# The normed rows of a graph layer turned by 32 x 32 blocks on VectorE and through DRAM, not by matmuls

## The chip, the cores and the metric

The kernel runs on one core of one Trainium2 chip. The time is the device time of that core in microseconds. The kernel before takes 1281.36 us, the median of three runs (1281.25 to 1281.46).

## The reference

Sixty-four graphs of 128 nodes with 256 features go through three layers with an attention over the neighbours and a feed-forward network:

```
h = relu(layernorm(x))                       # per node, 256 features
for l in range(3):
    si, sj = h @ attn_w[l, :256], h @ attn_w[l, 256:]
    scores = leaky(si[:, :, None] + sj[:, None, :] + attn_b[l])    # leaky slope 0.2
    attn = softmax(where(adj or diagonal, scores, -inf))           # 128 x 128 per graph
    y = layernorm(h + attn @ h) * g1[l] + beta1[l]
    ff = gelu(y @ W1[l] + b1[l]) @ W2[l] + b2[l]                   # 256 -> 1024 -> 256
    h = layernorm(y + ff) * g2[l] + beta2[l]
out = x + h
```

## The kernel before, in words

**Items and slots.** An item is four graphs in one layer (512 tokens); there are 48. Item q has layer q % 12 // 4, so four items of layer 0, four of layer 1 and four of layer 2 follow one another. Each engine's queue is written out by hand: a prologue for items 0 to 3, and then a function `slot(s)` for each s, in which an engine works on several items at once. In it `t` is item s - 1 (its second norm and output), `f` is item s (its feed-forward), `b` item s + 1, `a` item s + 2 and `d` item s + 3 (attention), and `p`, item s + 4, whose input is loaded and normed if it is of layer 0. Engines meet at semaphores alone, and each engine runs its queue in order.

**TensorE.** `ffn1(i, c)` makes 128 of the 1024 hidden features for 512 tokens: six matmuls of 512 columns (both operands split into a high and a low part) into one of three banks `hbank`. `ffn2(i, c)` adds that chunk's share of the output: twelve matmuls of 256 columns into two banks `acc`. An item's eight chunks of both are spread over a slot, and between them stand `e_turn` (four transposes of the exponentials E), `aggregate` (eight records, E by the rows x) and `z1_turn` (two times four transposes of the normed rows z, since ffn1 wants the features on the partitions). `e_turn` and `z1_turn` write the one bank `util`. `acc` has four banks, two for an item, so that one item's sums stand while the next item's are made; `aggregate` writes the banks of its item before ffn2 does.

**ScalarE.** `gelu_high` (gelu and a rounded copy) for each chunk, `h_high` (scale, shift and rounded copy of the turned z in `util`), `leaky`, `exps`, `et_out` (copy of the turned E), `first_x` (the input norm applied). Gelu and exp lie in different tables, so there are two table loads in a slot.

**VectorE.** `low` (the low part of a hidden chunk), `h_low` (the low part of the turned z), `j_dots` and `i_dots` (the products with the two attention vectors, four for each), `masked` (mask and sj row into the scores, one instruction), `minus_max`, `attend` (x plus the aggregate), `residual` (y plus ff), moments and norms. `variance` also adds epsilon (`ve`).

**GpSimd.** The power -0.5 (`make_rstd`) and the products and sums with the gamma and beta rows: `h_gamma`, `h_beta`, `x_gamma`, `x_beta`, `add_input`, each on two graphs (128x512). `h_gamma(i, h)` writes the ring `hb` of two items, and so waits for `residual(i - 2, h)`.

**DMA.** All DMAs stand in SyncE's queue. `send_sj` puts the sj values (16 bytes for each partition) into DRAM, and `load_sj` brings them back to all partitions.

Of the kernel before, what the change touches and what calls it, by code (L numbers as in the profile page):

```python
# [33 lines left out]
P = 128  # L34
# [12 lines left out]
LEAD = 3  # L47

# [3 lines left out]
def build(nc, x, adj, attn_w, attn_b, W1, b1, W2, b2, g1, beta1, g2, beta2, out):  # L52
# [19 lines left out]
    with ExitStack() as ctx:  # L72
# [27 lines left out]
        ET = sb("ET", [P, GG, P])  # L100
        sj_bc = sb("sj_bc", [P, P, GG])
        sj_dram = nc.dram_tensor("sj_dram", [2, P, GG], F32).ap()
# [8 lines left out]
        dots = sb("dots", [P, 2, GG])  # L111
        si = sb("si", [P, GG])
# [7 lines left out]
        ve = {n: sb(f"ve{n}", [P, GG]) for n in "012"}  # L120
        rstd = {n: sb(f"rstd{n}", [P, GG]) for n in "012"}
# [13 lines left out]
        acc = [psum(f"acc{i}", [P, HG, D]) for i in range(4)]  # L135
        util = psum("util", [P, TOK])

        def acc_of(i, h): return acc[2 * (i.q % 2) + h]
# [28 lines left out]
        zt_n = sem("zt_n")  # L167

# [13 lines left out]
        si_n = sem("si_n")  # L182
        pen_n = sem("pen_n")
        mask_n = sem("mask_n")
        negm_n = sem("negm_n")
# [33 lines left out]

        def x_of(i):  # L220
            return xs[:, i.q % XR]
# [28 lines left out]

        def wait_ring(eng, q):

            if q >= XR:
                eng.wait_ge(zt_n, KD * (q - XR + 1))
                eng.wait_ge(hgam_n, 2 * (q - XR + 1))
# [3 lines left out]
        def _(sp):  # L259
# [32 lines left out]
            def load_adj(i):  # L292
                wait(sp, pen_n, i.g)
                sp.dma_start(adji[:], group(adj, i.g)).then_inc(adj_in, 16)

            def load_weights(n):
                l, w, h = halves[n]
# [4 lines left out]
            def send_sj(i):  # L302
                sp.wait_ge(dotj_n, i.q + 1)
# [3 lines left out]
            def load_sj(i):  # L307
                sp.wait_ge(sj_sent, 16 * i.q)
# [3 lines left out]

            def slot(s):
                t, o, d, p = item(s - 1), item(s - 2), item(s + 3), item(s + 4)
                if p and p.l == 0:
                    load_xraw(p)
                if 6 <= s + 5 < len(halves):
                    load_weights(s + 5)
                if s == ITEMS - 4:
                    sp.wait_ge(x0_n, GG * NG)  # L320
                    sp.dma_start(xraw[:], group(x, NG - 1)).then_inc(last_in, 16)
                if o and o.l == L - 1 and o.q < ITEMS - 1:
                    for h in range(2):
                        gs = slice(h * HG, (h + 1) * HG)
                        sp.wait_ge(out_ready, 2 * o.g + h + 1)
                        sp.dma_start(group(out, o.g)[:, gs], xout[:, o.g % 2, gs]).then_inc(out_sent[o.g % 2], 16)
                if t and t.l == L - 1 and t.q < ITEMS - 1:
                    wait(sp, out_ready, 2 * t.g)
                    if t.g == 0:
                        sp.wait_ge(ln1_ready, 1)  # L330
                    sp.dma_start(xres[:], group(x, t.g)).then_inc(xres_in, 16)
                if p and p.l == 0:
                    load_adj(p)
                if d:
                    send_sj(d)
                    load_sj(d)

            load_xraw(item(0))
# [10 lines left out]
            load_xraw(item(2))  # L349
            load_adj(item(1))  # L350
            load_ln2_rows()
            load_attn_rows(False)
            load_weights(4)
            send_sj(item(1))
            load_sj(item(1))
            load_adj(item(2))
            load_weights(5)
            load_adj(item(3))
            load_xraw(item(3))
            send_sj(item(2))  # L360
            load_sj(item(2))
            for s in range(0, ITEMS + 3):
# [10 lines left out]
        def _(pool):  # L373
# [9 lines left out]
            def make_rstd(n, q):  # L383
                if n == "2" and q == ITEMS - 1:
                    return
                pool.wait_ge(ve_n[n], q + 1)
                if n == "0":
                    wait(pool, x0_n, GG * q)
                pool.tensor_tensor(rstd[n][:], ve[n][:], halfs[:], ALU.pow).then_inc(rstd_n[n], 1)  # L389
# [52 lines left out]
            def last_rstd(i):  # L442
                for h in range(2):
                    gs = slice(h * HG, (h + 1) * HG)
                    pool.wait_ge(ve_n["2"], i.q + h + 1)
# [11 lines left out]
            def slot(s):  # L457
                o, t, f, b, d = item(s - 2), item(s - 1), item(s), item(s + 1), item(s + 3)
                if o and o.l == L - 1:
                    add_input(o, 0)  # L460
                if o:
                    x_beta(o, 1)
                if d and d.l == 0:
                    make_rstd("0", d.g)
                if o and o.l == L - 1:
                    add_input(o, 1)
                if t:
                    make_rstd("2", t.q)
                if f:
                    h_beta(f, 0)  # L470
                if t:
                    x_gamma(t, 0)
                if f:
                    h_beta(f, 1)
                if b:
                    make_rstd("1", b.q)
                    h_gamma(b, 0)
                if t:
                    x_beta(t, 0)
                    x_gamma(t, 1)  # L480
                if b:
                    h_gamma(b, 1)
# [5 lines left out]
            make_rstd("0", i1.g)  # L488
            make_rstd("1", i0.q)
# [618 lines left out]
```

## Time and profile before

| what | value |
|---|---|
| median of three runs | 1281.36 us |
| the profiled execution: its time, its span | 1281.6 us, 1279.8 us |
| TensorE's granted clock, mean | 0.997 of full speed |
| busy: TensorE, VectorE, ScalarE, GpSimd | 97%, 87%, 72%, 51% of the span |
| prologue, until the first ffn1 has its second operand | 34 us |

Busy is the union of an engine's instructions. A matmul's record reaches over the start of the next one, so the distance between starts is what a matmul costs, and a busy share near 100% says that it never waited. The span is 1.8 us shorter than the profiled execution's own time.

### The profile page before, as it was taken

How to read it: one execution, taken by the hardware profiler on the slowest of the kernel's cores; microseconds unless marked ns; L12 is line 12 of the kernel's file. 1: busy time of each engine (PE TensorE's matmuls, PEld its weight loads, DVE VectorE, ACT ScalarE, POOL GpSimd, SP SyncE). 2: the span in 40 equal slices, each digit the busy share in tenths (PEclk: the TensorE clock that was granted, in tenths of full speed). 3: DMA queues.
4: the chain of work that ended last, by engine and by line, in shares of the span. 5: the costliest groups of instructions: out<-in, count | busy, mean ns of one | idle time of the engine just before them, and what ended most of it. 6: DMA issues, size and time to landing. Idle time of an engine off the chain costs nothing.

```text
span 1279.8 us, 23042 instructions
## 1 busy us (share of the span) xinstructions
PE 1240.6 (97%) x7877; PEld 1122.5 (88%) x7877; DVE 1110.3 (87%) x3331; ACT 917.7 (72%) x1754; POOL 652.5 (51%) x535
## 2 busy tenths in 40 slices
PE   3899999999999999999999999999999999999997
PEld 1799999988899999999889999999989899989996
DVE  7888888899998788889998888789999888888765
ACT  4777777677876776678777776777778766776663
POOL 1435553556555534554566445544666355435563
PEclk9999999999999999999999999999999999999998
DMA  7111111112220001011230000002321100000111
GB/s 248 53 33 43 26 26 34 34 51 66 67 67 10 10 10 17 10 34 51 75 100 26 9 18 10 9 10 43 99 75 42 34 10 9 10 17 26 26 41 58
DMA packets 52944, 52.31 MB, mean 41 GB/s; under 512 B 9272, under 2 KB 45148, under 8 KB 52828
## 3 DMA queue, kind: packets, MB, share of 16 engines
q1 hardware_dynamic: 52828, 50.85, 14.4%
q8 instruction: 62, 1.02, 0.3%
q14 instruction: 54, 0.44, 0.1%
HBM read 42.36 MB, written 8.48 MB: 40 GB/s over the span
## 4 chain that ended last, share of the span: by engine, by line
PE 77%; DVE 18%; ACT 2%; issue 2%; DMA 1%; POOL 0%; DVEq 0%; POOLq 0%
PE acc L955 35%; PE hbank L940 33%; PE acc L969 5%; DVE hid_lo L541 3%; PE util L990 3%; DVE xs L680 2%; PE util L1000 1%; DVE xs L667 1%; DVE st L528 1%; DVE st L674 1%; DVE ve L519 1%; DVE mv L517 1%; DVE st L562 1%; DVE junk L627 1%; DVE sc L654 1%
## 5 line engine op out<-in xcount | busy, mean ns | idle before, releaser
L955 PE MATMUL acc<-w2hi,hid_hi 128*128 128x256 f32 x1536 | 446.0, 290 | 0.0
L813 ACT ACTIVATE hbank<-hbank,vec 128x512 f32<-128x512 f32 x384 | 253.7, 661 | 266.5 <-PE hbank L940 262.0
L955 PE MATMUL acc<-w2hi,hid_lo 128*128 128x256 f32 x1536 | 434.9, 283 | 0.0
L955 PE MATMUL acc<-w2lo,hid_hi 128*128 128x256 f32 x1536 | 434.4, 283 | 0.0
L389 POOL TENSOR_TENSOR rstd<-ve,halfs 128x4 f32<-128x4 f32 x111 | 120.1, 1082 | 492.1 <-DVE ve L519 487.2
L940 PE MATMUL hbank<-ht_hi,w1hi 128*128 128x512 f32 x768 | 311.2, 405 | 2.8 <-DVE hid_lo L541 1.4
L955 PEld LDWEIGHTS acc<-w2hi,hid_hi 128*128 128x128 f32 x1536 | 293.8, 191 | 10.5
L940 PE MATMUL hbank<-ht_lo,w1hi 128*128 128x512 f32 x768 | 302.6, 394 | 0.0
L955 PEld LDWEIGHTS acc<-w2lo,hid_hi 128*128 128x128 f32 x1536 | 293.7, 191 | 8.8
L940 PE MATMUL hbank<-ht_hi,w1lo 128*128 128x512 f32 x768 | 300.8, 392 | 0.0
L955 PEld LDWEIGHTS acc<-w2hi,hid_lo 128*128 128x128 f32 x1536 | 293.5, 191 | 0.0
L541 DVE TENSOR_TENSOR hid_lo<-hbank,hid_hi 128x512 fp32r<-128x512 f32 x384 | 257.5, 683 | 26.5 <-ACT hid_hi L819 24.7
L819 ACT CAST hid_hi<-hbank 128x512 fp32r<-128x512 f32 x384 | 225.6, 587 | 13.7 <-PE acc L955 1.7
L409 POOL TENSOR_TENSOR hb<-xs,ln_rows 128x512 f32<-128x512 f32 x96 | 128.9, 1343 | 87.2 <-DVE xs L680 87.2
L940 PEld LDWEIGHTS hbank<-ht_hi,w1lo 128*128 128x128 f32 x768 | 144.7, 188 | 32.6
L940 PEld LDWEIGHTS hbank<-ht_hi,w1hi 128*128 128x128 f32 x768 | 145.7, 190 | 25.6 <-DVE ht_lo L685 2.1
L940 PEld LDWEIGHTS hbank<-ht_lo,w1hi 128*128 128x128 f32 x768 | 145.9, 190 | 19.9
L685 DVE TENSOR_TENSOR ht_lo<-util,ht_hi 128x512 fp32r<-128x512 f32 x96 | 66.2, 689 | 95.1 <-ACT ht_hi L836 95.1
L416 POOL TENSOR_TENSOR hb<-hb,ln_rows 128x512 f32<-128x512 f32 x96 | 124.5, 1298 | 0.0
L680 DVE TENSOR_SCALAR xs<-xs,mv,rstd 128x256 f32<-128x256 f32 x192 | 112.0, 646 | 1.0 <-POOL rstd L389 0.9
L829 ACT ACTIVATE util<-util,vec 128x512 f32<-128x512 f32 x96 | 72.4, 754 | 36.1 <-PE util L990 35.9
L426 POOL TENSOR_TENSOR xs<-xs,ln_rows 128x512 f32<-128x512 f32 x64 | 82.7, 1292 | 23.4 <-DVE xs L570 23.4
(76 smaller groups left out, 1740.3 us busy)
## 6 DMA issues: line engine op xcount, KB each, us to landing
sj_bc<-sj_dram SPq DMA_DIRECT2D x47, 256.0 KB, 3.9
xraw<-in_x_dram SPq DMA_DIRECT2D x16, 512.0 KB, 4.4
out_dram<-xout SPq DMA_DIRECT2D x32, 256.0 KB, 4.4
xres<-in_x_dram SPq DMA_DIRECT2D x15, 512.0 KB, 5.6
xout<-in_L_gnn_W_dram SPq DMA_DIRECT2D x10, 512.0 KB, 5.0
adji<-in_adj_dram SPq DMA_DIRECT2D x16, 256.0 KB, 2.9
ln_rows<-in_L_gnn_g_dram SPq DMA_DIRECT2D x2, 384.0 KB, 8.0
ln_rows<-in_L_gnn_beta_dram SPq DMA_DIRECT2D x2, 384.0 KB, 7.6
```

The costliest lines, as they stand in the source:

```text
L389: pool.tensor_tensor(rstd[n][:], ve[n][:], halfs[:], ALU.pow).then_inc(rstd_n[n], 1)
L409: pool.tensor_tensor(hb[:, i.q % 2, gs], x_of(i)[:, gs], rows_of(ln1_rows[:, 0], i.l), ALU.mult).then_inc(hgam_n, 1)
L416: pool.tensor_tensor(t, t, rows_of(ln1_rows[:, 1], i.l), ALU.add).then_inc(hb_n, 1)
L426: pool.tensor_tensor(t, t, rows_of(ln2_rows[:, 0], i.l), ALU.mult).then_inc(gam_n, 1)
L541: dve.tensor_tensor(hid_lo[:, k % HID], hbank[k % HB][:], hid_hi[:, k % HID].bitcast(F32), ALU.subtract).then_inc(lo_n, 1)
L680: dve.tensor_scalar(x_of(i)[:, g], x_of(i)[:, g], mv["1"][:, g, 0:1], rstd["1"][:, g:g + 1], ALU.subtract, ALU.mult).then_inc(z1_n, 1)
L685: dve.tensor_tensor(ht_lo[:, i.q % 2, m], util[:], ht_hi[:, i.q % 2, m].bitcast(F32), ALU.subtract).then_inc(htlo_n, 1)
L813: act.activation(hbank[k % HB][:], hbank[k % HB][:], ACT.Gelu, bias=b1c(i.l, c)).then_inc(gelu_n, 1)
L819: act.copy(hid_hi[:, k % HID], hbank[k % HB][:]).then_inc(hi_n, 1)
L829: act.activation(util[:], util[:], ACT.Identity, bias=beta1c(i.l, m), scale=g1c(i.l, m)).then_inc(ht_n, 1)
L940: mm = pe.matmul(hbank[k % HB][:], w[:, i.l, m, at_c], v[:, i.q % 2, m], start=m == 0 and n == 0, stop=m == KD - 1 and n == 2)
L955: mm = pe.matmul(to, v[:, k % HID, of_g], w[:, i.l, c], start=c == 0 and n == 0 and g % HG == 0, stop=c == C - 1 and n == 2, skip_group_ch ...
```

## The change

The turned rows of item 0 and 1 are still made by TensorE. For items 2 to 47 VectorE transposes z in 32 x 32 blocks (`turn_z`, one instruction over 128x1024), SyncE writes the result to a DRAM scratch of 512 KB (`send_z`) and reads it back in four DMAs, one for each group of 32 partitions, so that the blocks land turned as a whole in `zt` (`move_z`); `h_out` reads `zt` in place of `util`. `e_turn` writes a bank of the aggregation (`mix`), no longer `util`. The banks are dealt out anew: two `acc` for ffn2, in place of four, and two `mix` for E and the aggregation. So `ffn2(f, 0)` waits for both `residual` of the item before, and aggregation for the `attend` before.

`masked` is four instructions that add the mask and give the row's largest value as well, and `minus_max` works with four values for each partition, no longer with the 128x512 scores; it needs `penalty` to be cut off at 0 by a second instruction. The attention bias goes into `i_dots`. Epsilon is added on GpSimd. `input_shift` is one instruction, not four. And the order of every queue is written anew:

```
     def acc_of(i, h): return acc[h]
     def mix_of(i, h): return mix[h]
...
+            def send_z(i):
...
+                sp.wait_ge(tz_n, moved(i.q))
+                wait(sp, zt_in, MOVES_Z * (moved(i.q) - 1))
+                sp.dma_start(z_dram, tz[:].rearrange("p c g t -> p (c g t)")).then_inc(z_sent, 16)
...
+            def move_z(i):
...
+                sp.wait_ge(z_sent, 16 * moved(i.q))
+                sp.wait_ge(ht_n, KD * i.q)
+                for b in range(NQ):
+                    sp.dma_start(zt[b * QD:(b + 1) * QD].rearrange("p m a g t -> p m a (g t)"),
+                                 z_dram.rearrange("(a p) (m b f) -> b p m a f", a=NQ, b=NQ, m=KD)[b]).then_inc(zt_in, 16)
...
             def make_rstd(n, q):
...
-                pool.wait_ge(ve_n[n], q + 1)
+                pool.wait_ge(mv_n[n], GG * (q + 1))
...
+                pool.tensor_scalar(ve[n][:], mv[n][:, :, 1], EPS, None, ALU.add).then_inc(ve_n[n], 1)
...
             def masked(i):
...
-                dve.tensor_tensor(sc[:], pen[:, i.g % PENS], row, ALU.min).then_inc(mask_n, 1)
+                for g in range(GG):
+                    last = dve.tensor_tensor_reduce(sc[:, g], pen[:, i.g % PENS, g], row[:, g], 1.0, -BIG, ALU.add,
+                                                    ALU.max, msj[:, g, 0:1])
...
             def minus_max(i):
-                dve.wait_ge(leaky_n, GG * (i.q + 1))
-                dve.tensor_reduce(negm[:], sc[:], AX_X, ALU.max, negate=True).then_inc(negm_n, 1)
+                dve.scalar_tensor_tensor(out=below[:, :, 0], in0=msj[:, :, 0], scalar=-1.0, in1=si_of(i), op0=ALU.mult,
+                                         op1=ALU.subtract).then_inc(below_n, 1)
+                dve.wait_ge(below_n, i.q + 1)
+                dve.scalar_tensor_tensor(out=negm[:], in0=below[:, :, 0], scalar=SLOPE, in1=below[:, :, 0], op0=ALU.mult,
+                                         op1=ALU.min).then_inc(negm_n, 1)
...
+            def turn_z(i):
...
+                dve.wait_ge(z1_n, GG * (i.q + 1))
+                wait(dve, z_sent, 16 * (moved(i.q) - 1))
+                dve.transpose(tz[:], x_of(i).rearrange("p g (c j) -> p c g j", j=QD)).then_inc(tz_n, 1)
...
             def ffn2(i, c):
                 if c == 0:
-                    pe.wait_ge(y1_n, GG * (i.q + 1))
+                    wait(pe, y2_n, 2 * i.q)
```

In VectorE's prologue `penalty(i1)` and `input_moments(i2)` now stand right behind the first item's `masked`, ahead of its `attend`; TensorE's takes `e_turn` and `aggregate` of item 1 ahead of the second `z1_turn` of item 0.

VectorE's queue about the two `residual` of an item, before. `xs<-acc,hb` are they, the rows ahead of them `j_dots`, those behind `i_dots`; `si` is the attention bias, `hid_lo` a `low`, and `st<-xs` the moments:

```order
L620 ISA dots 128x1
L555 TENSOR_TENSOR xs<-acc,hb 128x512 [waits hgam_n,hb_n,zt_n,ffn2_n]
L555 TENSOR_TENSOR xs<-acc,hb 128x512 [waits hb_n]
L627 ISA junk,dots<-xs,attn_rows 128x256 [waits dotj_n]
L627 ISA dots 128x1
```

And now. `tz<-xs` is `turn_z`, `sc,msj` the new `masked`, and `below` and `negm` the new `minus_max`; `xout<-acc,hb` is `residual` of an item of layer 2, which writes the output tile:

```order
L729 ISA sc,msj<-pen,sj_bc 128x128
L729 ISA msj 128x1
L615 TENSOR_TENSOR hid_lo<-hbank,hid_hi 128x512 [waits hi_n]
L629 TENSOR_TENSOR xout<-acc,hb 128x512 [waits hb_n,out_sent1,ffn2_n]
L737 SCALAR_TENSOR_TENSOR below<-msj,dots 128x4 [waits exp_n,dots_n,mask_n]
L740 SCALAR_TENSOR_TENSOR negm<-below 128x4 [waits below_n]
L629 TENSOR_TENSOR xout<-acc,hb 128x512 [waits hb_n]
L636 BN_STATS st<-xout 128x6 [waits y2_n] x4
L592 MEMSET fence 128x1 [waits st2_n]
```

The two small instructions of `minus_max` have moved in between the two residuals, and the dots have moved to the middle of the slot. SyncE's queue in its prologue, before. `ln_rows` are the rows of the second norm, and `attn_rows` the attention vectors of layers 1 and 2:

```order
L290 DMA xraw<-in_x_dram 128x4x256 [waits x0_n]
L294 DMA adji<-in_adj_dram 128x4x128 [waits pen_n]
L283 DMA ln_rows<-in_L_gnn_g_dram 128x768
L284 DMA ln_rows<-in_L_gnn_beta_dram 128x768
L273 DMA attn_rows<-in_L_gnn_attn_w_dram 128x1024
```

And now:

```order
L313 DMA ln_rows<-in_L_gnn_g_dram 128x768
L314 DMA ln_rows<-in_L_gnn_beta_dram 128x768
L303 DMA attn_rows<-in_L_gnn_attn_w_dram 128x1024
L320 DMA xraw<-in_x_dram 128x4x256 [waits x0_n]
L324 DMA adji<-in_adj_dram 128x4x128 [waits edge_n] x2
```

The adjacency of item 1 (the first `adji`) has moved behind 1.25 MB of rows.

## Rows read from the trace of the kernel before

**Rows 1.** The page: the span, and busy time of each engine.
```profile
span 1279.8 us, 23042 instructions
PE 1240.6 (97%) x7877; PEld 1122.5 (88%) x7877; DVE 1110.3 (87%) x3331; ACT 917.7 (72%) x1754; POOL 652.5 (51%) x535
```

**Rows 2.** Groups by line, TensorE's transposes of z.
```profile
L990 PE MATMUL util<-ident,xs 128*128 128x128 f32 x384 | 59.2, 277 | 11.2 <-DVE xs L680 5.9 <-DVE ht_lo L685 5.2
```

**Rows 3.** Timeline of TensorE about one group: start, length, instruction.
```profile
162.70 0.28 PE L955 MATMUL acc<-w2hi,hid_lo 128*128 128x256 f32 x1
162.82 0.60 PE L990 MATMUL util<-ident,xs 128*128 128x128 f32 x4
163.18 0.36 PE L955 MATMUL acc<-w2hi,hid_hi 128*128 128x256 f32 x1
163.38 0.28 PE L955 MATMUL acc<-w2lo,hid_hi 128*128 128x256 f32 x1
```

**Rows 4.** Two slots: starts of two aggregations, then busy time by window.
```profile
404.85 0.38 PE L969 MATMUL acc<-xs,ET 128*128 128x256 f32 x1
430.43 0.81 PE L969 MATMUL acc<-xs,ET 128*128 128x256 f32 x3
...
425.80:451.38 25.58, 25.58 (x166) 23.29 (x166) 21.37 (x64) 18.25 (x36) 12.49 (x10) 1.00 0.06 11
599.53:625.85 26.32, 26.28 (x169) 23.70 (x168) 26.02 (x80) 20.56 (x41) 15.78 (x14) 1.00 0.27 81
```

**Rows 5.** Timeline at the boundary of an item, TensorE and VectorE.
```profile
451.31 0.28 PE L955 MATMUL acc<-w2hi,hid_lo 128*128 128x256 f32 x1
451.63 0.69 DVE L555 TENSOR_TENSOR xs<-acc,hb 128x512 f32<-128x512 f32 x1 [0.50 <-PE acc L955]
...
605.28 0.40 PE L940 MATMUL hbank<-ht_hi,w1hi 128*128 128x512 f32 x1
606.07 1.27 DVE L555 TENSOR_TENSOR xout<-acc,hb 128x512 f32<-128x512 f32 x2
607.27 0.41 DVE L627 CUSTOM_DVE_ANT_0 junk<-xs,attn_rows 128x256 bf16<-128x256 f32 x1
608.03 0.60 PE L1000 MATMUL util<-ident,sc 128*128 128x128 f32 x4
```

**Rows 6.** Timeline of VectorE and GpSimd where they meet.
```profile
603.03 1.30 POOL L455 TENSOR_TENSOR xout<-xout,xres 128x512 f32<-128x512 f32 x1
603.15 1.47 DVE L620 CUSTOM_DVE_ANT_0 junk<-xs,attn_rows 128x256 bf16<-128x256 f32 x1
...
620.72 1.40 POOL L409 TENSOR_TENSOR hb<-xs,ln_rows 128x512 f32<-128x512 f32 x1 [2.44 <-DVE xs L680]
620.88 1.38 DVE L680 TENSOR_SCALAR xs<-xs,mv,rstd 128x256 f32<-128x256 f32 x1
```

**Rows 7.** Groups by line, VectorE: count, busy us, mean ns, idle before.
```profile
L654 DVE TENSOR_TENSOR sc<-pen,sj_bc 128x512 f32<-128x512 bf16 x47 | 51.0, 1085 | 0.4 <-DMA sj_bc<-sj_dram 0.4
L658 DVE TENSOR_REDUCE negm<-sc 128x4 f32<-128x512 f32 x48 | 32.4, 676 | 1.8 <-ACT sc L842 1.8
L510 DVE TENSOR_TENSOR w1lo<-xout,w1hi 128x1024 fp32r<-128x1024 f32 x6 | 7.3, 1218 | 0.7 <-ACT w1hi L808 0.7
```

**Rows 8.** Median us of DMAs from issue to landing, with their size.
```profile
sj_bc<-sj_dram SPq DMA_DIRECT2D x47, 256.0 KB, 3.9
...
out_dram<-xout SPq DMA_DIRECT2D x32, 256.0 KB, 4.4
```

**Rows 9.** The prologue: two windows (last column GB/s), an issue, and the last ht_lo of item 0.
```profile
0.00:12.00 12.00, 1.16 (x5) 0.90 (x5) 5.77 (x29) 4.30 (x6) 2.16 (x10) 1.00 0.77 269
12.00:24.00 12.00, 5.68 (x14) 3.25 (x12) 9.57 (x32) 7.36 (x19) 1.01 (x1) 1.00 1.01 356
...
12.50 2.46 SPq L283 DMA_DIRECT2D ln_rows<-in_L_gnn_g_dram  x1
...
33.46 0.69 DVE L685 TENSOR_TENSOR ht_lo<-util,ht_hi 128x512 fp32r<-128x512 f32 x1
```

More of the change, by code:

```diff
@@ L334, in slot, with load_last_input @@
+            def load_last_input():
+                sp.wait_ge(x0_n, GG * NG)
+                sp.dma_start(xraw[:], group(x, NG - 1)).then_inc(last_in, 16)
+            def slot(s):
+                t, a, d, q6 = item(s - 1), item(s + 2), item(s + 3), item(s + 6)
                 if d:
                     send_sj(d)
+                if t and t.l == L - 1:
+                    load_xres(t)
+                if d:
                     load_sj(d)
+                load_weights(s + 6)
+                if a:
+                    send_z(a)
+                if q6 and q6.l == 0:
+                    load_adj(q6)
+                if a:
+                    move_z(a)
+                if t and t.l == L - 1:
+                    send_out(t, 0)
+                if q6 and q6.l == 0:
+                    load_xraw(q6)
+                if t and t.l == L - 1:
+                    send_out(t, 1)
+                if s == ITEMS - 4:
+                    load_last_input()
@@ L338, in _ @@
+            i1, i2, i3 = (item(q) for q in range(1, 4))
             load_xraw(item(0))
@@ L348, in _ @@
             load_weights(3)
-            load_xraw(item(2))
-            load_adj(item(1))
             load_ln2_rows()
             load_attn_rows(False)
+            load_xraw(i2)
+            load_adj(i1)
+            load_adj(i2)
             load_weights(4)
-            send_sj(item(1))
-            load_sj(item(1))
-            load_adj(item(2))
-            load_weights(5)
[L358 to L362, printed above, removed]
+            send_sj(i1)
+            load_sj(i1)
+            send_sj(i2)
+            load_sj(i2)
+            load_adj(i3)
+            load_xraw(i3)
+            send_sj(i3)
+            load_sj(i3)
+            load_weights(5)
+            send_z(i2)
+            load_weights(6)
+            move_z(i2)
+            for s in range(1, ITEMS + 3):
                 slot(s)
@@ L716, in slot @@
                 if a:
-                    masked(a)
-                if b:
-                    norm1(b)
+                    attend(a, 0)
                 if f:
                     low(f, 4)
-                if p and p.l == 0:
-                    input_moments(p)
                 if b:
                     h_low(b, 0)
+                if a:
+                    attend(a, 1)
                 if f:
                     low(f, 5)
+                if a:
+                    moments1(a)
+                if d:
+                    j_dots(d)
+                if b:
+                    h_low(b, 1)
+                if f:
                     low(f, 6)
+                if d:
+                    i_dots(d)
+                if f:
                     low(f, 7)
                 if a:
-                    minus_max(a)
+                    norm1(a)
+                if n and n.l == 0:
+                    input_moments(n)
+                if a:
+                    turn_z(a)
                 if b:
-                    h_low(b, 1)
+                    low(b, 0)
                 if d:
-                    j_dots(d)
-                if p and p.l == 0:
-                    input_shift(p)
-                if f:
-                    residual(f, 0)
-                split_weights(s + 4)
+                    masked(d)
+                if b:
+                    low(b, 1)
             i0, i1, i2, i3 = (item(q) for q in range(0, 4))
@@ L1005, in slot @@
                 if f:
-                    ffn2(f, 6)
-                    ffn2(f, 7)
+                    ffn1(f, 3)
+                    ffn1(f, 4)
+                    ffn2(f, 0)
+                    ffn2(f, 1)
+                if a:
+                    e_turn(a)
+                if f:
+                    ffn1(f, 5)
+                if a:
+                    aggregate(a, 0)
+                    aggregate(a, 1)
+                if f:
+                    ffn2(f, 2)
+                    ffn1(f, 6)
+                    ffn1(f, 7)
+                    ffn2(f, 3)
+                    ffn2(f, 4)
+                    ffn2(f, 5)
                 if b:
```

449 lines of the change are left out of this document (230 added, 219 removed).

## The prediction

> **What bounds the kernel now.** I read the page first: TensorE is busy 1240.6 of 1279.8 us, VectorE 1110.3 [rows 1]. Then the windows of single slots, since a mean over the span hides which slots are full. In a quiet slot (no input work, layer 0 or 1) TensorE is busy 25.58 of 25.58 us and VectorE 21.37; aggregations start 25.58 apart [rows 4]. The reader is to see that TensorE never waits there, so the slot costs what its matmuls cost. In the other kind of slot, in which an item of layer 0 comes in and one of layer 2 goes out, VectorE is busy 26.02 of 26.32 [rows 4]: there VectorE sets the pace. The excess over 25.58 in all such slots is small: z1_turn's whole idle time is 11.2 us, of which about 6 lie in the slots after the prologue [rows 2], and I take 6.
>
> **What is removed from TensorE.** A ffn2 matmul starts 0.12 after the one before. About a group of four transposes the matmul ahead starts at 162.70 and the second one behind it at 163.38: 0.68, of which 0.24 is two matmuls' own time, so a group costs 0.44 [rows 3]. Two groups for each of 46 items (2 to 47): 92 x 0.44 = 40.5 us. The 6 us of waits for the shared bank go with them. TensorE's floor for a slot is then 25.58 - 0.88 = 24.70.
>
> **What is added to VectorE.** turn_z is not in the trace. Its lower bound is a pass at one element in each step, the rate of the 128x1024 subtraction, 1.22 us with 1.13 of it on the queue [rows 7]; its upper bound is twice that, 2.3, if the blocks fill and drain in turn. I take 1.13. The Trainium skill (VectorE: DVE Perf Modes, The three transpose paths) gives 311 ns for 128x128 bf16 in 32 x 32 blocks; eight times the elements at one a cycle would be an estimated 1.25 us, near the lower bound; no row here shows it. masked was 1.09 [rows 7]; four products of 128 columns cost between half a dots instruction (0.34 from start to start of one, so 0.21) and that with the slow strided row (0.31): 0.85 to 1.25, I take 1.25. minus_max falls from 0.6 (its record 0.68) [rows 7] to 0.3, epsilon and bias leave (-0.4). The sum is 21.37 + 1.13 + 0.25 - 0.3 - 0.4 = 22.05, before collisions.
>
> **Collisions with GpSimd.** A product issued at 603.15, 0.12 behind a GpSimd product, took 1.47 in place of 0.41 [rows 5], till that one's end; the same with norm1's fourth instruction at 620.88 [rows 6]. So a VectorE instruction with two inputs on chip, or a norm, waits for a GpSimd instruction that is under way. The Trainium skill (SBUF — State Buffer, Who interferes with whom) calls this an exclusive lock on a shared pair of ports, and the trace agrees. Norm1's collision (1.0 us each item) goes: h_gamma(a) comes in the next slot and waits for residual(t). But then it starts exactly at the slot's head, where minus_max now stands. Work it through from the last ffn2 matmul's start, 0: residual(t, 0) starts at 0.32 (451.31 to 451.63) [rows 5], frees the queue after 0.60 (two of them take 1.27) and ends at 1.01; GpSimd starts h_gamma at 1.09; the first small instruction has run at 0.92, the second waits for the first's result and then for GpSimd, till 1.09 + 1.29 = 2.38. residual(t, 1) ends at 3.0. TensorE has two ffn1 chunks as cover, 605.28 to 608.03, 2.75 us [rows 5], so ffn2(f, 0) would be due at 2.87. It waits 0.2, and a restart costs it 0.1: 0.3 a slot. Without the collision residual(t, 1) would end at 1.9 and nothing wait. This is the term of four `acc` banks made two. A second collision: norm2(t, 1) meets x_gamma(t, 0), 0.8. VectorE's slot is then 22.05 - 1.0 + 1.1 + 0.8, and with some 0.7 of waits for ScalarE and GpSimd, 23.6. A quiet slot stays TensorE's: 24.7 + 0.3 = 25.0. Quiet slots are 26: 26 x 0.3 = 7.8 us.
>
> **The slots with more work.** In 12 slots an input comes in: the penalty (now two instructions) and the shift fall in the wait for norm2's power, but input_moments, 1.85, stands later: 23.6 + 1.85 = 25.5, which is 0.8 above the floor. 12 x 0.8 = 9.6. In 8 more (layer 2 alone) add_input meets masked; 25.2, 0.5 above: 4.0.
>
> **DMA.** send_sj and load_sj take some 6 together, 3.9 of it the second [rows 8]; masked follows j_dots by 6.3, so they are just hidden. send_z is 512 KB to DRAM: out_dram's 256 KB take 4.4 [rows 8], so at least 4.4 and at most 8.8; I take 5. move_z: three further issues at 0.4, and the last lands as sj_bc does, 3.9. Z = 10.2 in all. h_high(b, 0) wants it about 11.5 after turn_z; hidden. Only the first item's comes late, 1 us.
>
> **Prologue.** adji of item 1 stood behind 5.1 MB of loads and is 0.25 itself: 3.2 MB at 269 GB/s till 12 us, the other 2.1 at 356, and 2 us to land put it at about 20 (an estimate). Now 1.25 MB more stands ahead, 3.5 us [rows 9]: about 23.4. Behind masked(i0), at 17, VectorE's queue holds penalty(i1), which waits for it, and behind it minus_max(i0), attend(i0) and all that leads to the first ffn1. From 23.4 the order written out gives 0.9 + 0.35 + 1.4 + 1.85 + 1.4 + 1.1 to attend(i0, 0) at 30.3; then split, masked(i1), attend, minus_max, moments, j_dots, penalty(i2), norm1 till 40.8; two turns through ScalarE with attend(i1) and i_dots between them: the last ht_lo at 48.3, in place of 33.46 [rows 9]. That is 14.8 late; but item 2's E, its aggregation and two ffn1 chunks of item 1 (2.2 + 2.75) are then done ahead, and the first item waited less: net +9.
>
> **Sum.** 1279.8 - 40.5 - 6 + 9 + 7.8 + 9.6 + 4 + 1 = 1264.7 of span. Around it lie 1.8 in the profiled execution (1281.6), whose median is 0.2 below, so 1266.
>
> **Rivals.**
> *Only TensorE's work counts.* The second small instruction gets in ahead of h_gamma (they are 0.1 apart), and the prologue costs half: 1266 - 7.8 - 2 - 4.5 - 3 = 1249. For it: GpSimd's records are rough at 0.1. Against it: rows 6 show a loss at 0.12.
> *VectorE becomes the bound; slower.* If turn_z costs 2.3, masked 1.8 and one more product in a slot meets GpSimd (1.1), VectorE's slot is 23.6 + 1.2 + 0.6 + 1.1 = 26.5 and every microsecond over 25.0 counts 46 times: 1266 + 46 x 0.9, some 1305 (the input slots take 1.8 more already in both). It decides from 25.9 on, where the whole gain is spent. For it: VectorE is already full in a fifth of the slots.
> *The way through DRAM is too long; slower.* From z's landing to the next turn_z lie h_high (1.4) and 11.4 of VectorE's queue (half an attend 0.8, six subtractions of 512 columns at 0.6, moments 1.85, dots 2.8, norm1 1.3, turn_z 1.1). The loop closes in 12.8 + Z; it passes 25.0 at Z = 12.2, and at Z = 13 a slot is 25.8: 1266 + 46 x 0.8 = 1303. Against it: 10.2 by the rows; for it: send_z's upper bound alone is 3.8 more.
> *No change.* A slot of 25.3 in all: the terms cancel, 1280.
>
> **How the numbers follow.** Chances: forecast 0.42, the first rival 0.18, VectorE 0.17, DRAM 0.13, no change 0.10. Within the forecast the span of its terms (0 to 0.5 a quiet slot, prologue 5 to 14, input slots 25 to 26.2) gives 1253 to 1278. For eight in ten I take 1246 to 1300, since the two slower cases hold 0.30. A measurement here tells about 0.2% (2.6 us) from nothing: faster 0.58, same 0.10, slower 0.32.
>
> **What would show it.** In the profile after: no L990-like group but for two items; a stream transpose of 1.2 us; TensorE waiting at each item's first ffn2 matmul for residual, 0.2 to 0.3; the second of minus_max's instructions taking over 1 us; VectorE waiting near 17 us for adji; the last ht_lo of item 0 near 48. Wrong it is if ScalarE waits for zt in each slot, if VectorE has no idle time in quiet slots, or if turn_z is 2 us or more.

## The result, and the profile after

The changed kernel takes 1242.59 us (median of 4 runs, 1241.6 to 1243.66) against 1281.39 us for the kernel before beside it: a ratio of 0.9697, 95% interval 0.9681 to 0.9714, so 3% faster. Predicted were 1266 us and a range from 1246 to 1300; the result lies 3.4 us below the range. The direction was right, the size was not. The first rival ("only TensorE's work counts", 1249) came nearer, though it was still 6.4 us too slow: it was right that the collision stays away, while its halved prologue did not come.

The page of the profiled execution (1241.6 us in all) answers to [rows 1]:

```profile
span 1239.8 us, 23072 instructions
PE 1196.4 (97%) x7509; PEld 1082.8 (87%) x7509; DVE 1075.9 (87%) x3568; ACT 920.0 (74%) x1754; POOL 677.4 (55%) x648
```

TensorE lost 44 us of busy time and keeps its share. VectorE got a new 1.2 us instruction 46 times and still fell by 34 us. Windows from the end of one item's ffn2 to the next (length, then busy time of TensorE, weight loads, VectorE, ScalarE, GpSimd), a quiet slot and an input slot, answer to [rows 4]:

```profile
449.60:474.24 24.64, 24.64 (x157) 22.47 (x157) 21.02 (x70) 18.41 (x36) 12.78 (x12) 1.00 0.19 54
276.52:301.28 24.76, 24.76 (x157) 22.38 (x157) 23.43 (x83) 20.03 (x39) 16.55 (x16) 1.00 0.37 108
```

The quiet slot fell from 25.58 to 24.65, the input slot from 26.32 to 24.76. TensorE is full in both. The head of a quiet slot, in the timelines of VectorE and GpSimd, answers to the second line of [rows 5]:

```profile
449.63 0.69 DVE L629 TENSOR_TENSOR xs<-acc,hb 128x512 f32<-128x512 f32 x1 [1.14 <-PE acc L1073]
450.24 0.15 DVE L737 SCALAR_TENSOR_TENSOR below<-msj,dots 128x4 f32<-128x4 f32 x1
450.43 0.17 DVE L740 SCALAR_TENSOR_TENSOR negm<-below 128x4 f32<-128x4 f32 x1
450.51 0.68 DVE L629 TENSOR_TENSOR xs<-acc,hb 128x512 f32<-128x512 f32 x1
...
450.47 2.55 POOL L487 TENSOR_TENSOR hb<-xs,ln_rows 128x512 f32<-128x512 f32 x2 [9.08 <-DVE xs L629]
```

Two things are to be seen. VectorE waits 1.14 us for TensorE before residual(t, 0), so its own queue is not what ends a quiet slot. And minus_max's second instruction starts 0.04 us ahead of GpSimd's h_gamma: the collision that the prediction charged for does not happen. TensorE's matmul that needs residual(t, 1)'s bank follows the one before at its usual distance:

```profile
451.95 0.39 PE L1058 MATMUL hbank<-ht_hi,w1lo 128*128 128x512 f32 x1
452.18 0.28 PE L1073 MATMUL acc<-w2hi,hid_hi 128*128 128x256 f32 x1
```

residual(t, 1) ends at 451.19, and where TensorE does wait for it, in the runs below, it starts again 0.15 after its end, so there are about 0.85 us of slack here. The groups by line show the turn, and the DMA issues (count, size, median us to landing) its way through DRAM, with those of [rows 8]:

```profile
L748 DVE STREAM_TRANSPOSE tz<-xs 128x1024 f32<-128x1024 f32 x46 | 56.9, 1237 | 1.1
...
z_dram<-tz SPq DMA_DIRECT2D x46, 512.0 KB, 2.6
zt<-z_dram SPq DMA_DIRECT2D x184, 128.0 KB, 2.8
sj_bc<-sj_dram SPq DMA_DIRECT2D x47, 256.0 KB, 3.9
...
out_dram<-xout SPq DMA_DIRECT2D x32, 256.0 KB, 3.0
```

From the end of turn_z to the last landing of zt pass 7.7 us (median of 46; 7.3 to 9.6). ScalarE never waits for zt. In the prologue one wait stands out, as forecast, in VectorE's timeline:

```profile
23.12 0.69 DVE L713 SCALAR_TENSOR_TENSOR pen<-adji,diag 128x512 bf16<-128x512 int32 x1 [6.66 <-DMA adji<-in_adj_dram]
...
45.84 0.69 DVE L776 TENSOR_TENSOR ht_lo<-util,ht_hi 128x512 fp32r<-128x512 f32 x1 [0.43 <-ACT ht_hi L941]
```

**Where the 40.0 us of span went**, from the ends of each item's ffn2 in both traces:

| term | measured | predicted |
|---|---|---|
| z's transposes off TensorE (46 slots, 25.58 to 24.65) | -42.8 | -40.5 |
| what slots above 25.58 had cost before | -6.2 | -6 |
| prologue and first z: first ffn2 ends at 77.48 for 65.45 (+12.0), the first slot is 1.65 longer, the last two 2.2 and 4.1 shorter by work done ahead | +7.4 | +10 |
| collision at the head of quiet slots | 0 | +7.8 |
| slots with more work (what they exceed 24.65) | +1.9 | +13.6 |
| tail | -0.3 | 0 |
| sum | -40.0 | -15.1 |

### The profile page after: what moved, and what is told of

Same layout as the page of the kernel before. It is cut to its first block, busy times and chain, and to the rows that moved or that the text cites. A ratio compares the mean times of both kernels' runs of the same rounds, so it can differ in the third digit from the quotient of the medians.

```text
span 1239.8 us, 23072 instructions
## 1 busy us (share of the span) xinstructions
PE 1196.4 (97%) x7509; PEld 1082.8 (87%) x7509; DVE 1075.9 (87%) x3568; ACT 920.0 (74%) x1754; POOL 677.4 (55%) x648
## 4 chain that ended last, share of the span: by engine, by line
PE 95%; DVE 3%; SPq 1%; DMA 1%; issue 0%; POOL 0%; ACT 0%; DVEq 0%; POOLq 0%
PE acc L1073 44%; PE hbank L1058 42%; PE mix L1087 7%; PE mix L1112 2%; DMA adji<-in_adj_dram 1%; DVE xs L757 0%; DVE junk L694 0%; DVE st L603 0%; DVE st L764 0%; SPq L313 0%; PE util L1104 0%; SPq L332 0%; DVE sc L729 0%; POOL rstd L467 0%; DVE hid_lo L615 0%
## 5 line engine op out<-in xcount | busy, mean ns | idle before, releaser
L1058 PE MATMUL hbank<-ht_hi,w1hi 128*128 128x512 f32 x768 | 305.7, 398 | 3.6 <-DVE hid_lo L615 2.0
L487 POOL TENSOR_TENSOR hb<-xs,ln_rows 128x512 f32<-128x512 f32 x96 | 122.5, 1298 | 291.4 <-DVE xs L629 252.1
L757 DVE SCALAR_TENSOR_TENSOR xs<-mix,rden,xs 128x256 f32<-128x256 f32 x192 | 83.7, 477 | 30.8 <-PE mix L1087 30.6
L465 POOL TENSOR_SCALAR ve<-mv 128x4 f32<-128x4 f32 x111 | 29.5, 266 | 128.8 <-DVE mv L594 128.7
L1087 PE MATMUL mix<-xs,ET 128*128 128x256 f32 x384 | 95.8, 394 | 0.7 <-ACT ET L961 0.7
```

The source lines that it names most:

```text
L465: pool.tensor_scalar(ve[n][:], mv[n][:, :, 1], EPS, None, ALU.add).then_inc(ve_n[n], 1)
L487: pool.tensor_tensor(hb[:, i.q % 2, gs], x_of(i)[:, gs], rows_of(ln1_rows[:, 0], i.l), ALU.mult).then_inc(hgam_n, 1)
L757: dve.scalar_tensor_tensor(out=x_of(i)[:, g], in0=mix_of(i, h)[:, g % HG], scalar=rden[:, g:g + 1], in1=x_of(i)[:, g], op0=ALU.mult, op1=A ...
L1058: mm = pe.matmul(hbank[k % HB][:], w[:, i.l, m, at_c], v[:, i.q % 2, m], start=m == 0 and n == 0, stop=m == KD - 1 and n == 2)
L1087: mm = pe.matmul(mix_of(i, h)[:, g % HG], turned, x_of(i)[:, g], start=g % HG == 0, stop=True, skip_group_check=True)
```

## The experiments

Each kernel is an edit of the changed one. Times are medians of 4 runs; those of the kernel before, on the same chip, were 1281.43, 1281.90, 1281.83 and 1281.50 in the four groups of runs. Differences are taken from the changed kernel's 1242.59, which was timed beside none of them, so differences under about 3 us are told from nothing only where the slots in the traces agree. Slots are counted from one end of ffn2 to the next. In the eleven traces with the changed kernel's prologue the first ffn2 ends between 77.4 and 78.1.

**Turn by TensorE again, within the new order.** In every slot the two groups of transposes come back:

```
-BY_PE = 2
+BY_PE = 48
 (TensorE's slot)
                     ffn2(f, 1)
+                if b:
+                    z1_turn(b, 0)
                 if a:
                     e_turn(a)
...
                 if f:
                     ffn2(f, 2)
+                if b:
+                    z1_turn(b, 1)
+                if f:
                     ffn1(f, 6)
```

> Everything of the change stays (E in the aggregation's bank, the new mask, the sj row, the prologue), but the normed rows are turned by TensorE again in every slot, four transposes and two groups a slot as before; the VectorE blocks and the DRAM detour are not used after the prologue either. Theory (the time left TensorE's slots because 92 transpose groups of 0.43 to 0.46 us left its queue): the 46 slots grow by 0.9 us each, +41 us, so 1280 to 1286 us. Rival (most of the gain is the end of the old waits and of the E turn on the shared bank): only a few us come back, 1245 to 1255 us.

Measured: 1288.59 us, ratio to before 1.0055 (1.0039 to 1.0072). That is 2.6 us above the range that was expected and refutes the rival. All slots between the first and the last two are 25.68 to 26.06 long, +1.04 for a quiet one where 0.9 was expected, and 0.11 longer than before the change; what makes the 0.11 stays open. The window of a quiet slot:

```profile
439.36:465.04 25.68, 25.68 (x165) 23.36 (x165) 19.86 (x69) 18.38 (x36) 12.75 (x12) 1.00 0.06 11
```

The rest of the change without the turn by VectorE is thus 7 us slower than the kernel before, about what the prologue costs net (7.4 in the table), since the 0.11 a slot and the waits of before that are gone cancel: the gain, 46 us, hangs on the eight transposes a slot. The rest did make VectorE's slot 1.5 us lighter (19.86 for 21.37 in [rows 4]), and the input slots no longer stick out: this is the room into which the turn then went.

**The collision at the slot's head.** Four runs. The first lets minus_max wait for GpSimd's h_gamma:

```
                 dve.wait_ge(dots_n, i.q + 1)
+                if i.q >= 3:
+                    dve.wait_ge(hgam_n, 2 * (i.q - 1) + 1)
```

> The changed kernel, in which the first instruction of minus_max also waits for GpSimd's first h_gamma of the slot, as if GpSimd always won the start at the slot's head. minus_max and residual(t,1) then begin about 1.3 us later in each of the 45 slots. The forecast's step (the delay of residual(t,1) holds ffn2(f,0), 0.3 us a slot): +14 us, 1256 us. If such a delay lay fully on TensorE's path it would be up to 1.3 us a slot, +58 us. Rival (the slack of 1.1 us that the trace of after shows between residual(t,1) and the matmul that needs its bank takes it): 0 to +5 us, 1242 to 1248 us.

Measured: 1289.56 us, +47, far above both the 14 us of the forecast's step and the rival; quiet slots 25.61, +0.96. The slack was overrun: TensorE's first ffn2 matmul now shows the wait.

```profile
443.76 0.36 PE L1075 MATMUL acc<-w2hi,hid_hi 128*128 128x256 f32 x1 [0.73 <-DVE xs L629]
```

This prices a late residual(t, 1) at the slot's head, three times the 0.3 forecast, but the added wait's own delay (0.2 us after the end of h_gamma) is in it, and it doesn't show that a collision would come. So the order was to be turned round by a tiny instruction, one or three of them:

```
                 if a:
+                    for r in range(1):                 # 3 in the run tiny3
+                        dve.memset(tiny[:, r:r + 1], 0.0)
                     minus_max(a)
```

> The changed kernel with one tiny instruction of VectorE (a memset of one element a partition, 0.06 us) between residual(t,0) and minus_max in every slot. In the trace of after the second instruction of minus_max starts 0.04 us ahead of GpSimd's h_gamma. Theory (who starts first at the slot's head has the port, so 0.06 us more turns the order round and VectorE waits for the end of h_gamma, some 1.3 us later, of which 0.85 us is slack): about +0.45 us in 45 slots, +20 us, 1262 us. Rival (there is no such collision for operands of four elements a partition, or both engines work side by side): within 1 us of 1242.6.

> The same with three tiny instructions, 0.18 us. Theory (order turned round for certain): about +20 us, 1262 us, in the quiet slots 25.1 for 24.65 and VectorE's instruction held until h_gamma ends. Rival (no collision): residual(t,1) 0.18 us later, inside the slack, 1242 to 1244 us.

Measured: 1242.10 and 1242.42 us, no change. This looked like the rival's result, but the timelines say that the runs did not test it. Medians over the slots, from the end of ffn2: minus_max's second instruction starts at 0.835 in the changed kernel, at 0.848 with one memset and at 0.865 with three; h_gamma starts at 0.874 to 0.875 in all. The memsets are hidden between the first instruction and the second, which waits for its result. With three, VectorE and then GpSimd in a quiet slot:

```profile
450.43 0.16 DVE L738 SCALAR_TENSOR_TENSOR below<-msj,dots 128x4 f32<-128x4 f32 x1
450.44 0.08 DVE L786 MEMSET tiny<- 128x1 f32 x3
450.63 0.16 DVE L741 SCALAR_TENSOR_TENSOR negm<-below 128x4 f32<-128x4 f32 x1
...
450.63 2.57 POOL L488 TENSOR_TENSOR hb<-xs,ln_rows 128x512 f32<-128x512 f32 x2 [9.08 <-DVE xs L630]
```

The order was turned round in none of the 45 slots; with three memsets some 0.01 us is left between the two starts, and still nothing is held. A real 0.3 us was needed, with a control that has the same work one place later:

```
                 if a:
+                    dve.bn_stats(stx[:], attn_rows[:, a.l, 1])
                     minus_max(a)
                 if t:
(in the control, in place of the line above:)
+                    dve.bn_stats(stx[:], attn_rows[:, t.l, 1])
                     residual(t, 1)
```

> The changed kernel with one more instruction of VectorE in every slot between residual(t,0) and minus_max: moments of a constant 256-element row, 0.31 to 0.33 us. The runs tiny1 and tiny3 moved minus_max by 0.01 and 0.03 us only and did not turn the order round. This one puts both instructions of minus_max behind the start of GpSimd's h_gamma (it starts 0.87 us after the end of ffn2). Theory (whoever starts first at the slot's head has the port): VectorE is held to the end of h_gamma, residual(t,1) comes 1.4 to 1.5 us later, of which 0.85 us is slack, +0.6 us in 45 slots, about +27 us, 1270 us, and the input slots more. Rival (such small instructions do not collide with h_gamma): residual(t,1) comes 0.33 us later, inside the slack; the input slots, where VectorE's queue sets the end, take the 0.33 us, 12 of them: +3 to +5 us, 1246 to 1248 us.

> The same instruction behind minus_max, just ahead of residual(t,1): the control for the run head_stats, with the same work and minus_max ahead of h_gamma as in the changed kernel. Both theories: residual(t,1) 0.33 us later, inside the slack of 0.85 us, and 0.33 us on 12 input slots: 1246 to 1248 us. More than that would mean that the moments instruction, or residual(t,1) itself, is what GpSimd's h_gamma holds up.

Measured: 1273.78 us with the order turned round, 1242.25 us for the control. The same instruction costs 31.5 us in one place and nothing in the other. The timelines of the first, VectorE, then GpSimd, then TensorE:

```profile
460.99 0.69 DVE L630 TENSOR_TENSOR xs<-acc,hb 128x512 f32<-128x512 f32 x1 [1.14 <-PE acc L1075]
461.60 0.42 DVE L785 BATCH_NORM_STATS2 stx<-attn_rows 128x6 f32<-128x256 f32 x1
461.93 1.21 DVE L738 SCALAR_TENSOR_TENSOR below<-msj,dots 128x4 f32<-128x4 f32 x1
463.17 0.17 DVE L741 SCALAR_TENSOR_TENSOR negm<-below 128x4 f32<-128x4 f32 x1
463.25 0.68 DVE L630 TENSOR_TENSOR xs<-acc,hb 128x512 f32<-128x512 f32 x1
...
461.82 1.29 POOL L488 TENSOR_TENSOR hb<-xs,ln_rows 128x512 f32<-128x512 f32 x1 [9.08 <-DVE xs L630]
...
463.31 0.39 PE L1060 MATMUL hbank<-ht_hi,w1lo 128*128 128x512 f32 x1
464.08 0.35 PE L1075 MATMUL acc<-w2hi,hid_hi 128*128 128x256 f32 x1 [0.39 <-DVE xs L630]
464.27 0.28 PE L1075 MATMUL acc<-w2lo,hid_hi 128*128 128x256 f32 x1
```

An instruction on four elements a partition takes 1.21 us instead of 0.15, till the end of h_gamma. It started 0.11 us behind it. TensorE's matmul comes 0.77 after the one before instead of 0.23, and the next 0.19 behind it instead of 0.12: 0.61 a slot, and quiet slots are 25.25 to 25.27 long. In the control residual(t, 1) starts 0.34 later, within the slack, and the moments instruction runs beside h_gamma at its normal 0.42:

```profile
450.43 0.16 DVE L741 SCALAR_TENSOR_TENSOR negm<-below 128x4 f32<-128x4 f32 x1
450.51 0.42 DVE L787 BATCH_NORM_STATS2 stx<-attn_rows 128x6 f32<-128x256 f32 x1
450.85 0.67 DVE L630 TENSOR_TENSOR xs<-acc,hb 128x512 f32<-128x512 f32 x1
...
450.47 2.55 POOL L488 TENSOR_TENSOR hb<-xs,ln_rows 128x512 f32<-128x512 f32 x2 [9.09 <-DVE xs L630]
```

The control also cost the input slots nothing that can be measured, against the 3 to 5 us that both theories gave it: VectorE's wait for ScalarE's hid_hi, which stands behind the added instruction, falls there from 0.79 to 0.48 us and takes it.

**More work on VectorE.** Four instructions (eight in the second run) between norm1 and turn_z in every slot:

```
+                    for r in range(1):                 # 2 in the run stats2
+                        for g in range(GG):
+                            dve.bn_stats(stx[:, r, g], attn_rows[:, a.l, 1])
                     turn_z(a)
```

> The changed kernel with four more instructions of VectorE in every slot between the first norm and the turn (moments of a constant 256-element row into a tile that nobody reads; 0.31 us each from start to start), +1.25 us of VectorE's work a slot: 22.3 in a quiet slot and 24.7 to 24.8 in an input slot, of 24.65. The forecast's step (what is added goes straight onto VectorE's loop of 23.5 us from one residual to the end of its queue): quiet slots 24.75, so +0.1 to 0.3 on 26 of them, and +1.25 on the 20 others, +28 to +33 us, 1271 to 1276 us. Rival (VectorE's own waits shrink first, and only work above a slot's 24.65 counts): 0 to +10 us, 1243 to 1253 us.

> The changed kernel with eight such instructions a slot, +2.5 us: 23.5 us of VectorE's work in a quiet slot, 26.0 in an input slot, 24.5 to 25 in the layer-2 slots that have the output's. The forecast's step (straight onto the loop): quiet slots 26.0, so +1.35 on 26, +2.5 on 20, +85 us, 1328 us. Rival (only work above a slot's 24.65 counts): +0.1 to 0.2 on the quiet ones, +1.4 on the 16 input slots, +22 to +30 us, 1265 to 1273 us.

Measured: 1257.84 and 1305.17 us, +15.3 and +62.6: both between the theories. Windows of a quiet and an input slot of the first, then of the second:

```profile
455.14:479.79 24.65, 24.65 (x158) 22.48 (x157) 22.15 (x75) 18.44 (x36) 12.79 (x12) 1.00 0.18 54
579.77:605.81 26.04, 25.62 (x157) 22.30 (x156) 24.70 (x87) 20.11 (x39) 16.68 (x16) 1.00 0.37 102
```

```profile
445.06:470.69 25.63, 25.34 (x157) 22.23 (x157) 23.38 (x79) 18.26 (x35) 12.78 (x12) 1.00 0.18 52
600.60:627.94 27.34, 25.63 (x156) 22.30 (x156) 26.00 (x91) 20.10 (x39) 16.65 (x16) 1.00 0.33 97
```

The first 1.3 us costs a quiet slot nothing and an input slot all of it (24.75, 26.04, 27.34: 1.3 each time). So the 12 input slots of the changed kernel were already VectorE's, by a tenth, although TensorE shows busy there. The second 1.3 us costs the quiet slots 0.98. In VectorE's queue the waits before an instruction (over 0.12 us, by slot) give the reason. Changed kernel, quiet: 1.15 for TensorE at residual(t, 0), 0.90 for GpSimd's rstd, 0.46 for ScalarE's hid_hi, 0.96 for TensorE's mix; input slot: 0.80 for hid_hi and 0.34 for mix, no others. The loop without the wait at residual is 23.50 in the quiet slot; the input slot has 2.4 us more work, its waits shrink by 1.2, and it is 24.75. Neither theory holds, neither the one that adds all work to the loop nor the one that counts only work above a slot: in the input slots 1.13 of waits remain, whatever work is put behind them in the slot. Where it is put counts, as the control above shows.

**A longer way through DRAM.** The store is issued twice (three times in the second run), one after the other:

```
-                sp.dma_start(z_dram, tz[:].rearrange("p c g t -> p (c g t)")).then_inc(z_sent, 16)
+                for n in range(2):
+                    wait(sp, z_sent, 16 * (2 * (moved(i.q) - 1) + n))
+                    sp.dma_start(z_dram, tz[:].rearrange("p c g t -> p (c g t)")).then_inc(z_sent, 16)
...
```

> The changed kernel with the send of the turned rows issued twice, one after the other, so that the detour from the end of VectorE's turn to the last landing grows from 9.2 us to about 12 us. The forecast's step (hidden up to a detour of 12.2 us, then each us costs a us a slot): 0 to +10 us, 1243 to 1252 us. Rival (ScalarE's h_out was just in time already): +2.7 us in 46 slots, above 1340 us.

> The changed kernel with the send of the turned rows issued three times, one after the other: the detour grows from 9.2 to about 15 us. The forecast's step (hidden up to 12.2 us, then a us a slot for each us): +2.8 us in 46 slots, about +130 us, 1370 us. Rival (more slack than 12.2, since h_out may come late as long as ffn1's first group has its two halves): less than half of that, below 1305 us.

Measured: 1249.76 us (+7.2), as the theory had it, and 1332.71 us (+90), between the 1370 of the theory and the rival's 1305. The 9.2 us in the expectation were one slot's; the medians are 7.7, 10.5 and 13.2 (so the theory's 15 was too long). With 10.5 the quiet slots are untouched, and the ones about the input slots, whose turn_z comes later in the slot, take up to 1.3 more. With 13.2 quiet slots are mostly 25.3 to 27 long, about the 26.0 that the forecast's "12.8 + Z" gives, and ScalarE waits for zt for each of the 46 items:

```profile
ACT util L936 <- DMA zt<-z_dram: 135.5, 46, 6.8
```

By the same formula the changed kernel's detour is hidden with 24.65 - 12.8 - 7.7 = 4.2 us to spare in a quiet slot. In an input slot the formula lacks a term: input_moments (1.85) stands ahead of turn_z too. An estimate with it, 12.8 + 1.85 + 13.2 = 27.9, fits the 27.0 to 29.0 of the input slots in send3.

**The mask as before.** One minimum over 128 x 512 and one maximum over its rows come back, and penalty loses its second instruction:

```
-                for g in range(GG):
-                    last = dve.tensor_tensor_reduce(sc[:, g], pen[:, i.g % PENS, g], row[:, g], 1.0, -BIG, ALU.add,
-                                                    ALU.max, msj[:, g, 0:1])
-                last.then_inc(mask_n, 1)
+                dve.tensor_tensor(sc[:], pen[:, i.g % PENS], row, ALU.min).then_inc(mask_n, 1)
...
+                dve.tensor_reduce(negm[:], sc[:], AX_X, ALU.max, negate=True).then_inc(negm_n, 1)
```

> The changed kernel with the mask of before: one minimum over 128 x 512 and one maximum over its rows instead of the four masked sums with their maxima, the two small instructions of minus_max and the penalty's minimum. VectorE's work a slot grows by about 0.2 us. Theory (VectorE isn't the bound, and minus_max is not on TensorE's path): within 2 us of 1242.6. Rival (the shorter instruction at the slot's head, 0.32 us for 0.68, is part of the gain because it comes ahead of residual(t,1)): +0.3 us a slot, +14 us, 1256 us.

Measured: 1241.44 us, 1.2 less than the changed kernel, no more than runs differ by, so the theory holds and not the rival. The slots show more: every one is 24.65 long, the input slots too, while the first ffn2 ends 1.7 later (79.22). The new mask gains in the prologue and loses as much in the input slots.

**Loads in another order, and a version that takes both.**

```
-            load_ln2_rows()
-            load_attn_rows(False)
             load_xraw(i2)
             load_adj(i1)
+            load_ln2_rows()
+            load_attn_rows(False)
```

> The changed kernel with the prologue's loads in another order: the raw rows of item 2 and the adjacency of item 1 go before the second norm's rows and the rest of the attention rows. Theory (VectorE's wait of 6.7 us for the adjacency of item 1 is what the prologue now costs): 3 to 6 us faster, 1237 to 1240 us. Rival (the prologue is held by the sum of its DMA traffic, and something else is late instead): within 1 us of 1242.6.

Measured: 1239.53 us, ratio to before 0.9672 (0.9658 to 0.9687), as the theory had it. The wait for the adjacency falls from 6.7 to 3.7 us and the first ffn2 ends 2.4 earlier. Then the mask in two forms, and the adjacency further ahead:

```
             def masked(i):
+                if i.q >= 3:
+                    dve.tensor_tensor(sc[:], pen[:, i.g % PENS], row, ALU.add).then_inc(mask_n, 1)
+                    return
             def minus_max(i):
+                if i.q >= 3:
+                    dve.wait_ge(leaky_n, GG * (i.q + 1))
+                    dve.tensor_reduce(negm[:], sc[:], AX_X, ALU.max, negate=True).then_inc(negm_n, 1)
+                    return
```

and, in the second kernel:

```
             load_weights(1)
+            load_adj(i1)
             load_b2_rows()
```

> The changed kernel with the prologue's loads as in the run adj_first, and with the mask in two forms: the first three items as in the changed kernel, the others by one sum over 128 x 512 and one maximum over its rows after the leaky step. Theory (the two gains are separate: 3.0 us of prologue, and about 1.9 us of input slots that the shorter VectorE queue gives back, without the 1.7 us that the old mask cost in the prologue): 1237 to 1238 us. Rival (they share what they gain): 1239 to 1240 us.

> The same, with the adjacency of item 1 loaded even before the second norm's bias and the first norm's rows, right behind the second piece of weights. Theory (VectorE still waits 3.7 us for it in the run adj_first, and this is the next thing late): 2 to 3 us faster than the run mixed_mask, 1235 us. Rival (the traffic only changes places, and the weights of item 0 are late instead): the same or slower, 1237 to 1241 us.

Measured: 1238.49 us (ratio to before 0.9662, 0.9648 to 0.9677) and 1239.53 us. The first is the fastest kernel here, 4.1 us under the changed one, between its theory and its rival. The loads alone gave 3.1 of that; the 1.0 beside it is within what can be told from nothing, though the slots agree with it. In it the first four input slots are up to 0.4 long, the others 24.65. Moving the adjacency further ahead brought nothing: the wait for the adjacency (3.8 us) is gone, but VectorE's waits for raw rows rise from 4.5 to 7.1 us and a wait for the sj rows from 0.2 to 2.5. So the rival holds in that the traffic only changes places; it is not the weights that come late.

## Why the prediction was wrong, step by step

- **What bounds the kernel, and the term of the transposes:** right. -42.8 us for -40.5; a group costs TensorE 0.465 of the slot rather than 0.44, and putting the two groups back cost 1.04 a slot.
- **VectorE's added work:** the price of turn_z was right (1.16 on the queue, 1.24 by its record, for 1.13). The estimate of 1.25 from the Trainium skill (VectorE: DVE Perf Modes, The three transpose paths) agrees with that record. VectorE's quiet slot was forecast as 22.05 - 1.0 + 1.1 + 0.8 = 22.95; it is 21.02. The 1.1 did not come and of the 0.8 next to nothing, as told below; without these two collisions the sum is 21.05. That it meets 21.02 so closely is partly luck. From start to start, i_dots and norm2 cost 0.47 more than before, which the sum left out, and minus_max, epsilon and bias, j_dots and the last step of the moments cost 0.51 less than it had. For masked the sum adds 0.25 where its own figures, 1.25 for 1.09, give 0.16; on the queue it is 1.23 for 1.00.
- **The collision at the slot's head, 7.8 us:** the step that failed in kind. The rule behind it, that a VectorE instruction with two inputs in SBUF waits for a GpSimd product under way, holds here even for four elements a partition, as head_stats shows (1.21 us for 0.15). The Trainium skill (SBUF — State Buffer, Who interferes with whom) states this rule, and the trace agrees. But the order was read wrong by 0.1 us: GpSimd starts 0.15 after residual's end, not 0.08 (450.47 for 450.32), and minus_max's second instruction starts 0.2 behind the first. The first rival named just this. With 0.04 us between the two starts, the rows of before could not settle it. The price was wrong as well, the other way: had it come, it would have been 0.6 in all 45 slots, not 0.3 in 26; 31 us by head_stats (45 times 0.61 is 27, the input slots lose more), and the change would have gained 0.6%.
- **The second collision, norm2 with x_gamma:** there, but next to nothing where 0.8 was forecast. A `low` and the wait ahead of it stand between the two halves of norm2, so the second half starts 1.0 us behind x_gamma (456.21 for 455.21) and is held for its last 0.05: the pair takes 0.78 for 0.74. The longest hold in any slot is 0.6 us, in three slots.
- **Slots with more work, 13.6 us:** the step that failed in size, 1.9 measured. The forecast took a loop of 23.6 and put all of input_moments on top, 25.5. The loop measured 23.50, but that agreement is luck: the forecast had 22.95 of work and 0.7 of waits, and there are 21.02 of work and 2.5 of waits. With waits taken as so few and fixed, nothing could give way. In fact the wait for the aggregation shrinks too, from 0.96 to 0.34, and the whole loop gains 1.25 (24.75). The 12 input slots lose 1.5 for 9.6 forecast. In slots with layer 2 alone masked does meet add_input (1.48 for 0.38 at the worst), but most of it falls into VectorE's waits: three such slots are 0.06, 0.30 and 0.11 over 24.65, the others none, 0.5 together for 4.0 forecast. The runs stats1 and stats2 show that VectorE does set the end of the input slots.
- **DMA:** hidden, as forecast. Z is 7.7 for 10.2; the store of 512 KB takes 2.6 where the rows of smaller stores gave a bound of 4.4. The formula for the loop was right for quiet slots, by send2 and send3, and lacked input_moments for the input slots. The 1 us for the first z shows in no wait.
- **Prologue:** right in place (the wait ends at 23.12 for 23.4 forecast) and nearly in size: the last ht_lo of item 0 starts at 45.84 for 48.3, and with the first z 7.4 for 10.
- **The range:** it allowed for two slower cases with 0.30 between them. Both were well off: VectorE had over a microsecond to spare in quiet slots, the detour over four. (The price of the first of them was also a slip: a slot of 26.5 is 1.5 over 25.0, and 46 x 1.5 on 1266 is 1335, not 1305, beyond the range.) All misses lay on one side, 24.9 us: 11.7 slots with more work, 7.8 collision, 2.6 prologue, 2.3 transposes, 0.5 in the old waits and the tail. Without the first two the forecast would have been 1246.5, just inside the range.

## What to carry to other kernels

When a bound engine hands work to a fuller-looking one, list the second engine's waits one by one in the slot and ask which of them will shrink; those that end by its own chain stay (here 1.13 of 3.5 us, for work put behind them). When two engines can collide, price both orders and find the start times to a few hundredths: here an order that holds by 0.04 us is worth 31 us, and nothing in the code keeps it. And when an experiment on such an order shows no change, look in its trace whether the order was turned round at all.

## What the runs showed of the hardware

- A VectorE instruction with both inputs in SBUF and four elements a partition is held by a GpSimd product that started 0.11 us ahead of it, 1.21 us for 0.15. One that started 0.04 us ahead of GpSimd is not. The residual (one input in a TensorE bank, 0.68 us) and the moments instruction (0.42) run beside the same GpSimd product at their normal lengths.
- The trace of before had such holds already. In 12 slots the epsilon instruction, 128x4 with one input, and h_gamma started within 0.015 us of each other, and epsilon took 1.32 us for 0.17, till the end of h_gamma. In one of them:

```profile
624.62 1.32 DVE L519 TENSOR_SCALAR ve<-mv 128x4 f32<-128x4 f32 x1
...
624.62 1.29 POOL L409 TENSOR_TENSOR hb<-xs,ln_rows 128x512 f32<-128x512 f32 x1
```

- At 0.01 us the recorded starts alone do not tell who is held: epsilon was held in four slots in which its record starts 0.002 to 0.011 us ahead of GpSimd's, and in tiny3 minus_max was not, 0.003 to 0.011 ahead. Whether the form of the instruction or the true order makes the difference, no run shows.
- A VectorE transpose of 128 x 1024 fp32 in 32 x 32 blocks takes 1.24 us, its queue 1.16.
- A store of 512 KB from the chip to DRAM lands in 2.6 us (median of 46), less than the 4.4 that the 256 KB of out_dram took in the trace of before; those take 3.0 now.
- Three small memsets between an instruction and the one that waits for its result moved the second by 0.03 us.
